# First attention of a six-stage kernel: softmax maxima carried as two rows of the score product, the DRAM fills issued earlier, and a batch's side work spread over other steps and engines

## What is computed

```python
q, k = apply_rope(elu(q) + 1), apply_rope(elu(k) + 1)       # 16 heads of 8 features, 256 tokens, 8 batches
attn = softmax(einsum('bhnd,bhmd->bhnm', q, k) * scale)
attn_out = einsum('bhnm,bhmd->bhnd', attn, v)
lepe = conv1d(v, w_lepe, padding=1, groups=c) + b_lepe      # three taps over the tokens
x = x + attn_out + lepe
```

## Time and profile before

| | |
|---|---|
| median of 3 runs | 1023.5 us (1023.48 to 1025.39) |
| the profiled execution's own time | 1016.72 us |
| its span in the profile | 1014.9 us |
| TensorE matmul busy | 864.3 us, 85% of the span |
| VectorE / ScalarE / GpSimd busy | 738.9 / 534.7 / 284.7 us |
| granted TensorE clock, mean | 0.919 of full |
| stage a0 | 131 to 315.6 us of the span |

### The profile page before, as it was taken

How to read it: one execution, slowest core, us unless ns; L and a number is a source line. 1 busy time by engine, 2 the same in 40 slices (tenths; PEclk the granted TensorE clock), 3 DMA queues, 4 the chain that set the end, 5 groups by cost and what they waited for, 6 DMA issues and landing times.

```text
span 1014.9 us, 23408 instructions
## 1 busy us (share of the span) xinstructions
PE 864.3 (85%) x7494; PEld 657.2 (65%) x7494; DVE 738.9 (73%) x2619; ACT 534.7 (53%) x1452; POOL 284.7 (28%) x395
## 2 busy tenths in 40 slices
PE   5889989999996899957789378999999998669892
PEld 4457856666764457745789246676767766548892
DVE  7768888878867866986646658877787788468455
ACT  4233044556654413113557427877887888425564
POOL 3034035624101002207755270000000000057762
PEclk9999995999997899975989779999999999959997
DMA  9204079810004505034540246454645462163414
GB/s 250 60 1 141 1 275 374 267 57 1 2 1 108 135 1 141 1 115 136 161 107 29 93 132 201 138 175 126 188 127 180 128 191 85 41 191 79 114 39 128
DMA packets 134949, 119.77 MB, mean 118 GB/s; under 512 B 10755, under 2 KB 115227, under 8 KB 134836
## 3 DMA queue, kind: packets, MB, share of 16 engines
q1 hardware_dynamic: 130292, 109.83, 36.7%
q0 software_dynamic: 4544, 8.54, 2.4%
HBM read 67.45 MB, written 51.80 MB: 117 GB/s over the span
## 4 chain that ended last, share of the span: by engine, by line
PE 62%; DVE 14%; ACT 10%; issue 5%; DMA 3%; SPq 2%; POOL 2%; DVEq 1%; POOLq 0%; ACTq 0%
PE psum L1602 6%; PE psum L970 6%; PE psum L979 6%; PE psum L1516 5%; PE psum L2720 4%; PE psum L2190 3%; PE psum L2769 3%; PE psum L2128 3%; ACT a_L L2850 3%; PE psum L2756 2%; ACT a_L L2848 2%; PE psum L747 2%; PE psum L2093 2%; PE psum L2736 2%; PE psum L1542 2%
## 5 line engine op out<-in xcount | busy, mean ns | idle before, releaser
L2348 DVE TENSOR_REDUCE a_negmax<-psum 128x2 f32<-128x512 f32 x128 | 83.8, 684 | 20.5 <-PE psum L2128 18.9
L2297 ACT ACTIVATE a_PT<-psum 128x1024 f32<-128x1024 f32 x64 | 65.5, 1023 | 26.8 <-PE psum L2173 26.5
L2850 ACT ACTIVATE a_L<-a_L,a_least 128x256 f32<-128x256 f32 x128 | 63.3, 495 | 0.0
L2720 PE MATMUL psum<-a_KT,a_Q 64*128 64x128 f32 (+1 forms) x512 | 57.6, 342 | 3.4 <-DVE a_least L2910 1.3
L1027 ACT ACTIVATE g_hT<-psum,g_wt 128x128 f32<-128x128 f32 x156 | 44.5, 368 | 25.1 <-PE psum L970 25.1
L2848 ACT ACTIVATE a_L<-a_L,a_least 128x128 f32<-128x128 f32 x128 | 50.6, 395 | 10.7 <-DVE a_least L2910 9.8
L1027 ACT ACTIVATE f_hT<-psum,f_wt 128x128 f32<-128x128 f32 x156 | 44.5, 368 | 22.0 <-PE psum L970 22.0
L2908 DVE CUSTOM_DVE_ANT_0 a_L<-psum,a_X 128x128 f32<-128x128 f32 x128 | 36.6, 286 | 25.0 <-PE psum L2720 24.9
L2167 PE MATMUL psum<-a_turned 24*128 24x256 f32 x256 | 54.2, 362 | 0.0
L2910 DVE CUSTOM_DVE_ANT_0 a_L<-psum,a_X 128x256 f32<-128x256 f32 x128 | 53.7, 420 | 0.0
L2128 PE MATMUL psum<-a_turned 24*128 24x256 f32 x224 | 51.6, 339 | 0.9 <-ACT a_turned L2263 0.7
(11 more groups left out here) (589 smaller groups left out, 2584.0 us busy)
## 6 DMA issues: line engine op xcount, KB each, us to landing
z<-a_G SPq DMA_DIRECT2D x32, 512.0 KB, 3.6
a_X<-z SPq DMA_DIRECT2D x16, 1024.0 KB, 6.8
f_slots_dram<-empty SPq DMA_DIRECT2D x1, 8910.0 KB, 28.1
g_slots_dram<-empty SPq DMA_DIRECT2D x1, 8910.0 KB, 51.6
a_X<-z SPq DMA_DIRECT2D x16, 512.0 KB, 4.1
f_wgu<-in_gate_up SPq DMA_DIRECT2D x16, 384.0 KB, 6.3
z<-pad SPq DMA_DIRECT2D x6, 1024.0 KB, 10.3
g_wgu<-in_gate_up SPq DMA_DIRECT2D x16, 384.0 KB, 6.9
```

What stands on the lines that cost most here:

```text
L2297: act.activation(PT[m % 4][:, :, :, :].rearrange("p j t n -> p j (t n)"), core.psum[:, 2 + 2 * (u % 2):4 + 2 * (u % 2), :], ACT.Exp, scale ...
L2348: dve.tensor_reduce(negmax[:, :, h], query_bank(b, h).rearrange("p (t n) -> p t n", n=SEQ), AX.X, ALU.max, negate=True).then_inc(max_done, 1)
L2720: last = pe.matmul(out, Q[rows, at, b % 2, queries], KT[rows, at, b % 2, keys], start=True, stop=True)
L2850: act.activation(pr[:, o, P:3 * P], L[:, o, P:3 * P], ACT.Exp, bias=least[:, o, 1:2], scale=-1.0, accum_out=sums[:, o, 1:2]).then_inc(p_re ...
```

## The change

**Maxima as two rows of the product.** The stacks of queries and keys get two more rows per head (24 and 25). On the keys' side they hold ones, set once by GpSimd. On the queries' side they hold the high part and the rest of the negated maxima, written by DMA from `shift`: per batch eight transfers of 4 rows by 256 numbers, issued by SP once ScalarE has copied the turned maxima. `by_key` then multiplies 26 rows, and the 0/1 matrix and its products are gone.

**Order.** In a step's first block TensorE puts the second head of the coming batch, by query, between the products by key, and the first head right behind them. The products of `values_and_convolution` are split in two halves (steps 2 and 4), `turn_maxima` moves from step 6 to 5, `project` from step 7 to 6 (in batch 0 it stays at 7), and the stacks are turned at steps 1, 3, 5 and 0. `take_out` and the copy of `shift` move from VectorE to ScalarE; the add of the attention to `x` moves from VectorE to GpSimd except for the last four groups, over four buffers of `attn`.

**Fills and borders.** The fills are issued at the end of f0's transfers instead of the start of a0; the borders are written one per batch between the maxima rows. The diff, cut to its core:

```diff
-    def write_pads(self, sp):
-        sp.wait_ge(self.pad_filled, 1)
-        for s in range(2):
-            for q in range(2):
-                ...
+    def write_pad(self, sp, i):
+        s, q, side = self.PADS[i]
...
     def sync(sp):
-        pass
+
+        for b in range(BATCH):
+            sp.wait_ge(shift_ready, b + 1)
+            for g in range(GROUPS):
+                for part in range(2):
+                    s = H0 * part + HG * g
+                    sp.dma_start(turned[b % NT][0][PARTS + part::HW, g, :],
+                                 shift[b % 2][s:s + HG, :]).then_inc(rows_written[b % 2][g], 16)
+            if b < len(Early.PADS):
+                core.early.write_pad(sp, b)
...
+        def by_key(b, u, j, t):
+            h = 2 * u + j
+            g, rows = h // HG, slice(HW * (h % HG), HW * (h % HG) + SHIFTED)
+            q, k = turned[b % NT]
+            return pe.matmul(bank[2 + 2 * (u % 2) + j][:, SEQ * t:SEQ * t + SEQ], k[rows, g, P * t:P * t + P].bitcast(F32R),
+                             q[rows, g, :].bitcast(F32R), start=True, stop=True)
...
-        def scores_by_key(b, u):
+        def scores(b, u, second):
             m = b * STEPS + u
-            if u == 0:
-                pe.wait_ge(shift_ready, b + 1)
+            if second:
+                place_for_query(*second, second_order(*second))
+                by_query(*second, 0)
+            if u % 2 == 0:
+                pe.wait_ge(rows_written[b % 2][u // 2], WRITES * (b // 2 + 1))
             if m >= 2:
                 pe.wait_ge(p_ready, m - 1)
-            q, k = turned[b % NT]
             for t in range(2):
+                if second and t:
+                    by_query(*second, 1)
                 for j in range(2):
-                    ...
-                for j in range(2):
-                    h = 2 * u + j
-                    rows = slice(HW * (h % HG), HW * (h % HG) + HW)
-                    last = pe.matmul(bank[2 + 2 * (u % 2) + j][:, SEQ * t:SEQ * t + SEQ], select[rows, h, :],
-                                     shift[b % 2][rows, :], start=False, stop=True, skip_group_check=True)
+                    last = by_key(b, u, j, t)
             last.then_inc(s2_done, 1)
...
                 if n == 0:
-                    pe.wait_ge(max_done, H0 + 4)
-                scores_by_key(i, u)
+                    pe.wait_ge(max_done, H0 + 6)
+                scores(i, u, due[1])
...
             for n, st in enumerate(made):
                 st["sync"](sp)
+                if names[n] == "f0":
+                    fills.sync(sp)
                 if names[n] == "a0":
-                    fills.sync(sp)
-                    core.early.write_pads(sp)
+                    fills.wait_emptied(sp)
+                    core.early.wait_pads(sp)
```

270 lines of the change are left out of this document (161 added, 109 removed).

## The result

| | before | after |
|---|---|---|
| median of the runs, us | 1024.45 (1023.48 to 1025.89, 4 runs) | 1007.9 (1006.11 to 1008.55, 4 runs) |
| ratio after/before | | 0.9845, 95% interval 0.9822 to 0.9868 |
| profiled execution, us | 1016.72 | 1006.11 |
| its span, us | 1014.9 | 1004.4 |

The change gains 16.5 us by the medians, and only 10.6 us between the two profiled executions.

What follows compares the result with a forecast made beforehand. TensorE was taken as the bound of a0, the one stage changed. Gains of 1.5 + 3.1 + 3 x 2.7 + 1.9 + 1.5 + 1.5 = 17.6 us over eight batches gave a median of 1006 us, range 1000 to 1014.

Steps and rivals of the forecast that it cites:

- The block: Each a0 step's small TensorE products: twelve become eight, 0.92 us falls to 0.66, bounds 0.56 and 0.79.
- a rival with 0.15: The eight products run as two rounds, block 0.56 us: 0.1 us more in 40 steps, 1002 us; chance 0.15.
- 2.1 us a batch: The shorter block's gain in a0: 0.26 us a step over a batch's eight steps.
- The 0.51 and 0.26 us: TensorE's waits for VectorE per batch, before the values and before the maxima are turned; both counted as gone.
- where I put 0.2: New TensorE waits per batch, for ScalarE's take-out before turning at step 0 and fp32 turning of maxima: 0.2 us lost.
- 8.1 + 1.9 + 1.5 + 1.5: Gains in us: batches 2 to 4 at 2.7 each, then batch 5, batch 6 and batch 7.
- The cap: Batches 6 and 7 gain only 1.5 us each: VectorE near its limit in 6, ScalarE limiting in 7.
- the wait of 1.48 gone, five steps at some 0.3: Batch 0: TensorE's wait for the copy of `shift` vanishes and steps shorten; less 1.5 us later start, 1.5 us gained.
- the clock's fall gone: Batch 1: the low TensorE clock at 188 to 192 us returns to 1.00, counted as 1.2 us gained.
- the clock stays low longer: Start waits keep TensorE at 1.2 GHz 6 to 8 us more in batch 0: 1010 us; chance 0.08.
- the maxima rows land late: Row transfers queue with borders on SP, landing 7.3 us too late in all eight batches: 1064 us; chance 0.05.
- The cover: 3.9 us between ScalarE's copy and step 0, to hide the first row pair's 2.4 to 3.8 us; cost 0.

Runs made afterwards that it cites:

- a_old_order: Changed kernel with the second head's query back at a step's end and its maximum last on VectorE; ratio to the old kernel 0.9949.
- a_extra: Changed kernel with four products of the removed ones' size put back into each step, in the new order; ratio to the old kernel 0.9932.
- b_no_select: Old kernel without its four products for the maxima in each step; 1060.69 us against 1062.59, ratio 0.9997.
- a_lumped: Changed kernel with a batch's values and convolution issued whole at step 4, not by halves at steps 2 and 4; ratio to the old kernel 0.9942.
- b_relief_no_select: Old kernel with output copy on ScalarE, add on GpSimd, and the maxima products left out; 1021.64 us, ratio 0.9981.
- a_turn_stats: Changed kernel with batch 0's maxima turned at step -2 and the statistics put behind the maxima in steps 0 to 2; ratio to the old kernel 0.9843.
- a_warm: Changed kernel with three unused TensorE products added at each of four steps in a0's opening; ratio to the old kernel 0.9865.
- a_start: Changed kernel with batch 0's maxima turned earlier, statistics moved behind maxima, and unused TensorE products added in the opening; 1004.99 us, ratio to the old kernel 0.9819.
- a_fills_late: Changed kernel with the DRAM fills issued as a0 starts, ahead of the maxima rows in SP's queue; one run, 1060.56 us.
- before_again: The old kernel unchanged, profiled a second time on the slower chip; 1061.88 us.
- b_relief: Old kernel with the copy of a group's output on ScalarE and its add on GpSimd, maxima products kept; 1023.99 us, ratio 0.9992.
- after_again: The changed kernel unchanged, profiled a second time on the slower chip; 1049.15 us, ratio to the old kernel 0.9893.

## Why the prediction was right, and where it was not

The median was predicted as 1006, within 1000 to 1014, and came out at 1007.9. The terms behind it were off in both directions.

**The block: right that it shrinks, mis-sized.** Predicted 0.66 us with 0.56 as the lower bound; measured 0.45. The step that failed is the choice "I take 0.66, not 0.56, because the new order ends with two products in one strip". `a_old_order` has 0.66 us to the hundredth, so the pace taken from the earlier trace rows holds for eight products in the old order. What the runs show in place of my reason: the two products that end the new order lie in a strip of their own, and start with the others (four products by 217.69, the other four by 217.91), so they cost nothing. The pace that I took was that of a block in which one strip gets six of the twelve products. The Trainium skill ("TensorE: Matmul & The Clock Gate", Part 3), which I made a rival with 0.15, pointed the right way: the trace agrees that the eight products are two rounds, and even passes the 0.56 us that I had worked out for it. `a_extra` shows it once more from the other side: twelve products, four in the fullest strip, in 0.69 us.

**"2.1 us a batch" of the block in the sum: right in size, wrong in kind.** I multiplied a gain per step by eight as if TensorE were alone. `b_no_select` refutes that: in the kernel before the deletion is worth 0.5 us in batch 2 and nothing in the total. Counted from before, the parts tried give 0.48 (deletion), 0.10 (VectorE's relief) and 0.71 (both). Counted back from after, they cost 0.90 (products put back), 0.57 (old order) and 0.97 (values in one piece). The difference to be explained is 3.35 us. So the parts are worth more the more of the others are there. The mechanism, as I read it from the traces: TensorE hands scores to VectorE and ScalarE step by step, and a batch had places at which these chains set the pace whatever TensorE saved: the values behind `a_attn` at step 0, the turning of the maxima, and the long stretch without scores. The spread over steps removes these places, and more of TensorE's saving arrives. Of these places only the long stretch has a run of its own (`a_lumped`); the others are argued. The step from `b_relief_no_select` (19.17) to the three a-kernels near 17.4 us holds pieces that I did not run apart: stacks turned every other step, the projection at step 6, and the maxima split and turned in another form. If order and split are worth their 0.57 and 0.97 us, 19.17 - 16.53 - 1.54 = 1.1 us a batch is in these pieces together. Which of them it is stays open.

**Waits: the old ones went, new ones mis-sized.** The 0.51 and 0.26 us of the earlier trace rows are gone as predicted, and no wait for `a_attn` is left. New in batch 2 are 0.75 us for `a_turned` at step 1 and 0.22 us for `a_OT`, 0.97 us where I put 0.2.

**Middle batches.** Batches 2 to 7 were to give 8.1 + 1.9 + 1.5 + 1.5 = 13.0 us and gave 3.35, 3.21, 2.25, 2.12, 0.84 and 0.33, together 12.1. The total is right because a block that gained nearly twice as much was offset by the new waits, and by batches 6 and 7, which gave less than the 1.5 us each. The cap that I put on them holds for ScalarE in batch 7: there TensorE waits 0.9 us for the exponentials and 1.0 us for ScalarE's `a_OT`. VectorE, which I took for the limit of batch 6, is busy 8.70 of its 14.4 us.

**Start and batches 0 and 1: wrong, by 6.9 us.** The way to the first exponential was to cost 1.5 us and cost 1.9; this part is right. But batches 0 and 1 were then to gain 3.0 and 3.1 us and lost 1.26 and gained 0.91. The steps that failed are "the wait of 1.48 gone, five steps at some 0.3" and "the clock's fall gone". The wait of 1.48 us did go, and six waits for VectorE's maxima, 4.7 us with the 1.58 at step 0, took its place, since a step's first product now depends on the maximum of the step before. The statistics between the maxima are a small part of it: `a_turn_stats` moves them away and 4.2 of the 4.7 us stay. In batch 1 the waits for an elu are of 1.59 and 0.96 us, where the one of 0.69 was to become 0.3 longer.

And the clock did not come back earlier, it dipped longer: it was low until some 180 us, not 175, and 0.78 on the mean from 180 to 204 us, where I expected 1.00; in the window from 188 to 192 us, which the prediction named, it was 0.66. In batch 1 it was 0.84 against 0.92 before, and it is 0.84 there in `a_warm`, `a_start` and `a_fills_late` too, each with a batch 1 of 21.25 us. That is the rival "the clock stays low longer", to which I gave 0.08. How the 6.9 us divide between waits and clock stays open.

**Rows, fills, borders: right at no cost.** The rows come in time because nothing else is in the queue. `a_fills_late` shows the rival "the maxima rows land late" at work: 14.3 us for one late pair, once. The early issue of the fills is thus a condition of the rows by DMA. The Trainium skill's "mostly overhead" ("DMA: Bandwidth & Descriptors", rules for kernel authors) agrees with the trace as far as this: SP spends 0.54 us and more on an issue of 4 KB, and nearly as little, 0.58, on a border of 1 MB. The cover hides it. When the rows land when nothing is ahead of them no view shows.

**Profile against median: open.** Of the 16.5 us the profiled pair shows 10.6. With 1.8 us of after's own distance to its median and 7.7 of before's the numbers close, but why before's executions are mostly 7 us slower than its profiled one I can only argue. The candidate is the stretch of low clock in a0. It lasted until about 175 us in the profiled execution of before; in `before_again`, and in `b_relief` on a chip of the faster kind, until about 192 us, and their a0 took 7.5 and 10.1 us longer. (In each, a shorter dip in batch 4 is part of that.) If most executions of before are like these, the medians close. The granted clock of whole executions points the same way: 0.919 in the profiled one, 0.907 to 0.916 in 19 of before that ran beside `a_start` (1022.38 to 1028.95 us). By an estimate from these, a mean of 0.910 in place of 0.919 is 18 us more at half clock in 1015; by its windows of 4 us `before_again` spends some 41 us of a0 at half clock where before spent 24. No trace of such an execution on the first chip exists. The predicted 17.6 us against 16.5 measured is therefore a better hit than its parts deserve, and in part luck: a0's parts as read were 9.8.

## What to carry to other kernels

Before counting n steps times what one removed product costs, mark the places in the loop where the engine waits or where it hands out nothing for a long time; a saving between two such places ends at the next one. Here deleting a third of the products gained nothing in the old schedule and nearly 1 us a batch in one whose other work was spread, so test a deletion in the schedule that it is meant for. When small products use different row strips of the array, count them by strip: here the fullest strip set the length of a block, and twelve products took as long as eight when it had four in both.

## What the runs showed of the hardware

*The low clock in a0 comes in two lengths, whatever the kernel.* In all 14 traces it fell between 152 and 160 us. In seven it was up again by 175 to 181 us (before, after, `a_extra`, `a_lumped`, `a_warm`, `a_start`, `a_turn_stats`), in the other seven not before 188 us (`before_again`, `after_again`, `a_old_order`, `a_fills_late`, all three other b-kernels). Before and after each have one trace of either kind. What TensorE did until then does not tell them apart: it was busy 13.92 us from 156 to 176 us in both traces of after. Windows of before:

```profile
156.00:176.00 20.00, 19.31 (x118) 13.47 (x116) 16.81 (x43) 8.26 (x11) 10.89 (x24) 0.52 1.03 374
176.00:188.00 12.00, 10.23 (x110) 6.96 (x105) 10.69 (x22) 7.15 (x10) 11.77 (x17) 1.00 0.73 259
```

and the same of `b_relief`:

```profile
156.00:176.00 20.00, 19.31 (x110) 13.34 (x110) 16.56 (x42) 8.17 (x12) 10.65 (x24) 0.50 1.02 374
176.00:188.00 12.00, 12.00 (x82) 8.29 (x86) 6.40 (x15) 5.23 (x8) 11.77 (x17) 0.50 0.73 259
```

TensorE is busy 19.31 of 20 us in both, and then runs at 2.4 GHz in one and at 1.2 GHz for 12 us more in the other, busy without a gap. Batch 0 takes 22.36 us in the one and 28.24 in the other: 5.9 us, a third of what the whole change gains, by something that no change tried here controls.

*The clock also dips in the middle batches, and less work for TensorE does not prevent it.* `b_no_select` and `b_relief_no_select` ran on chips of different kinds and both dip at the same places: in windows of 4 us the clock is 0.81 and 0.77 from 232 to 240 us in the one and 0.83 and 0.74 in the other, then 0.87 and 0.71 from 252 to 260, and 0.89 and 0.68. At the first of these places the clock is full in the three traces with the maxima products in the old schedule. The second is not theirs alone: `before_again` has 0.57 from 256 to 260 us, and `b_relief`, with all of its products, 0.64, 0.50 and 0.58 from 256 to 268, where batch 4 took 22.87 us in place of 18.34. So that the deletion brings the dips is likely for the first place only. In the new schedule there are none from 204 to 300 us in after, `a_extra`, `a_warm`, `a_start` and `a_lumped`. There are some in `a_old_order` and `a_fills_late`, before 220 us, and in `after_again` and `a_turn_stats`, where they cost 2.7 us in batch 2 and 1.4 in batch 3.
